# A graph transformer layer on one core: four moves at the seam between its two passes

## What is computed

```python
xn = layernorm(x)
# graph part: per edge an attention over 4 heads; node n takes the transformed row of dst[n]
xt    = xn @ weight                                   # 12500 x 256
alpha = softmax(leaky_relu(xt[src] . attn_l + xt[dst] . attn_r))   # per head
gnn   = sum_h alpha[n, h] * xt[dst[n], h]             # 64 values, repeated for 4 heads
# linear attention: K needs sums over ALL nodes before any message
Q, K  = elu(xn @ Wq) + 1, elu(xn @ Wk) + 1
msg   = layernorm(((Q @ (K^T V)) / (Q @ sum(K))) @ Wm) * g1 + b1
h     = relu(concat(xn, msg) @ W1) @ W2
x     = x + gnn + xn + layernorm(h) * g2 + b2
z     = layernorm(x)                                  # then a shared MLP and 4 experts, top 2
x     = x + shared(z) + gated_experts(z)
```

## Time and profile before

| | |
|---|---|
| median of 3 runs | 1385.67 us |
| lowest and highest | 1385.67 and 1386.52 us |
| the profiled execution | 1385.64 us, of which the span of the trace is 1383.9 us |
| mean granted TensorE clock | 0.993 |
| PE, DVE, POOL, ACT busy | 97%, 76%, 68%, 57% of the span |

### The profile page before, as it was taken

One profiled execution on the slowest core, in us unless ns is written; L12 is line 12 of the kernel. 1 busy time (PEld: TensorE's weight loads), 2 busy tenths in 40 slices (PEclk: granted clock), 3 DMA queues, 4 the chain that ended last, 5 costly groups with the idle time before them and its releaser, 6 DMA issues.

```text
span 1383.9 us, 27085 instructions
## 1 busy us (share of the span) xinstructions
PE 1342.4 (97%) x9032; PEld 1192.8 (86%) x9032; DVE 1049.1 (76%) x2617; ACT 791.4 (57%) x1439; POOL 943.2 (68%) x867
## 2 busy tenths in 40 slices
PE   5999999978999999999999999999999999999998
PEld 4999999866888888888888888888888888888876
DVE  6877777878787777877778777787777877788774
ACT  4555556335655656556565565555665566655565
POOL 4777766758766776677766777667766677667650
PEclk9999999989999999999999999999999999999999
DMA  5787767322212222112211122111221112212000
GB/s 166 254 272 240 241 213 248 116 58 65 68 32 60 69 75 67 30 52 75 75 58 40 53 75 73 44 52 55 75 71 41 56 56 75 71 31 67 4 16 30
DMA packets 71784, 121.81 MB, mean 88 GB/s; under 512 B 38082, under 2 KB 42815, under 8 KB 71752
## 3 DMA queue, kind: packets, MB, share of 16 engines
q1 hardware_dynamic: 55752, 108.00, 24.7%
q0 software_dynamic: 16000, 13.43, 4.5%
HBM read 69.47 MB, written 51.70 MB: 88 GB/s over the span
## 4 chain that ended last, share of the span: by engine, by line
PE 90%; DVE 3%; POOL 2%; issue 1%; DVEq 1%; ACT 1%; POOLq 1%; DMA 1%; SPq 0%; ACTq 0%
PE psum L228 27%; PE psum L229 27%; PE psum L230 27%; PE psum L438 5%; PE psum L518 1%; PE psum L511 1%; PE psum L608 1%; PE psum L707 1%; PE psum L692 1%; POOL xg L1788 1%; POOL ag L1790 1%; DVE base L1445 0%; DMA attn_bc<-in_L_gnn_attn_l 0%; POOL e_lo L1794 0%; POOLq L1727 0%
## 5 line engine op out<-in xcount | busy, mean ns | idle before, releaser
L228 PE MATMUL psum<-w_hi,h_hi 128*125 128x256 f32 x600 | 170.7, 285 | 0.6 <-DVE h_lo L1564 0.5
L230 PE MATMUL psum<-w_hi,h_lo 128*125 128x256 f32 x600 | 168.4, 281 | 0.0
L229 PE MATMUL psum<-w_lo,h_hi 128*125 128x256 f32 x600 | 168.2, 280 | 0.0
L1794 POOL TENSOR_TENSOR h_lo<-relu,h_hi 128x1000 fp32r<-128x1000 f32 x50 | 124.7, 2494 | 49.4 <-ACT h_hi L969 49.3
L1788 POOL DMA_INDIRECT xg<-table_xt,idx x100 | 125.0, 1250 | 39.4 <-issue 38.2
L1790 POOL DMA_INDIRECT ag<-table_al,idx x100 | 122.7, 1227 | 30.5 <-issue 30.5
L228 PE MATMUL psum<-z_hi,w_hi 128*128 128x500 f32 x300 | 121.5, 405 | 1.9 <-DVE z_lo L1573 1.0
L893 ACT ACTIVATE row_n<-psum,nm_m,rs_m 125x256 f32<-125x256 f32 x100 | 48.4, 564 | 127.4 <-POOL nm_m L1730 127.4
L228 PE MATMUL psum<-xT_hi,w_hi 128*128 128x500 f32 x300 | 120.3, 401 | 0.0
L229 PE MATMUL psum<-xT_lo,w_hi 128*128 128x500 f32 x300 | 117.4, 391 | 0.0
L230 PE MATMUL psum<-xT_hi,w_lo 128*128 128x500 f32 x300 | 117.1, 390 | 0.0
(11 more groups left out here) (273 smaller groups left out, 4613.2 us busy)
## 6 DMA issues: line engine op xcount, KB each, us to landing
xb<-in_x SPq DMA_DIRECT2D x50, 448.0 KB
xT_hi_table<-x1T_hi SPq DMA_DIRECT2D x25, 500.0 KB
xT_lo_table<-x1T_lo SPq DMA_DIRECT2D x25, 500.0 KB
xT_hi<-xT_hi_table SPq DMA_DIRECT2D x25, 500.0 KB, 3.9
xT_lo<-xT_lo_table SPq DMA_DIRECT2D x25, 500.0 KB, 4.8
table_xt<-xts SPq DMA_DIRECT2D x25, 455.0 KB
out<-xmid SPq DMA_DIRECT2D x24, 448.0 KB
xb<-in_x SPq DMA_DIRECT2D x50, 52.0 KB
```

Of the source, the lines that this page charges most:

```text
L228: pe.matmul(out, wh, xh, start=first, stop=False)
L229: pe.matmul(out, wh, xl, start=False, stop=False)
L230: return pe.matmul(out, wl, xh, start=False, stop=last)
L1794: ptt(out, src, hi, ALU.subtract).then_inc(S[done], 1)
```

## The change

Four moves, and a new order of tiles in memory that makes one of them legal:

1. DVE: `feature_high(0, 2)` comes after the copy of the key sums.
2. DVE: `second_parts(2)` moves from turn 0 (ahead of `soft_chain_in`) to turn 1 (behind `soft_chain_out`). It reads `w_raw`, memory of pass 1, so the tiles on that memory are now ones that pass 2 writes first in its turn 2 (`e1_hi`, `s2_hi`), and no longer `scaleT`, `mT_hi`, `mT_lo`.
3. POOL: in turn 1 `rstd` of y comes before the first gather of group 2, and `rstd` of z before the second.
4. PE: in turn 2 the two `w1_part` on the x of group 1 come ahead of the wait for `y` and the message's transposes, behind a wait for `m_norm` of group 1.

```diff
@@ tiles @@
-        scaleT = sb("scaleT", [P, GR], F32R)
-        mT_hi = sb("mT_hi", [P, CK, GR], F32R)
-        mT_lo = sb("mT_lo", [P, CK, GR], F32R)
+        e1_hi = sb("e1_hi", [P, 4, GR], F32R)
+        s2_hi = sb("s2_hi", [P, GR], F32R)
...
@@ PE, phase2 @@
+                def hidden_of_old_x():
+                    if x_ahead:
+                        pe.wait_ge(S["m_norm"], T * i)
+                    w1_part(0, 2, 6, xT_old)
+                    w1_part(0, 3, 7, xT_old).then_inc(S["xT_free"], 1)
...
                 if b:
 
+                    if x_ahead:
+                        hidden_of_old_x()
                     if due(i - 1):
                         pe.wait_ge(S["y"], i - 1)
                     transposes(row_n, 0, "mt", "m_norm", T * (i - 1))
-                    w1_part(0, 2, 6, xT_old)
-                    w1_part(0, 3, 7, xT_old).then_inc(S["xT_free"], 1)
+                    if not x_ahead:
+                        hidden_of_old_x()
...
-            phase2(2, 0, own_q=False)
+            phase2(2, 0, own_q=False, x_ahead=True)
@@ DVE, end of pass 1 @@
-            feature_high(0, 2)
             dve.wait_ge(S["hb_mm"], 1)
             dve.memset(kden[:], 0.0)
             dve.wait_ge(S["kx"], NG)
             dve.tensor_copy(kx[:], psum[:, 6:8, 0:KX_W]).then_inc(S["kxs"], 1)
+            feature_high(0, 2)
             dve.drain()
@@ DVE, turn0 and turn1 @@
                 feature_high(1, 2)
-                second_parts(2)
                 dve.drain().then_inc(S["p1_dve"], 1)
...
                 soft_chain_out(0, True, False)
+                second_parts(2)
                 over_den(1, 2)
@@ POOL, turn1 @@
                 rstd(LM, "mv_m", 2, "rs_m")
+                rstd(LY, "mv_y", 1, "rs_y")
                 pool.wait_ge(S["gnn"], 1)
                 pool.wait_ge(S["idx0"], 2 * dma16(2, 0))
                 gathers(0, (0,))
-                rstd(LY, "mv_y", 1, "rs_y")
+                rstd(LZ, "mv_z", 1, "rs_z")
                 gathers(0, (1,))
-                rstd(LZ, "mv_z", 1, "rs_z")
```

More of the change, by code:

```diff
@@ L187, in gps_layer @@
         s1_lo = sb("s1_lo", [P, 2, GR], F32R)
-        e1_hi = sb("e1_hi", [P, 4, GR], F32R)
+        scaleT = sb("scaleT", [P, GR], F32R)
+        mT_hi = sb("mT_hi", [P, CK, GR], F32R)
+        mT_lo = sb("mT_lo", [P, CK, GR], F32R)
         e1_lo = sb("e1_lo", [P, 4, GR], F32R)
-        s2_hi = sb("s2_hi", [P, GR], F32R)
         s2_lo = sb("s2_lo", [P, GR], F32R)
@@ L592, in w2_pair, with phase2 @@
                 last.then_inc(S["w2"], 1)
-            def phase2(i, par, a=True, b=True, c=True, own_q=True):
+            def phase2(i, par, a=True, b=True, c=True, own_q=True, x_ahead=False):
                 xT, mT, zT = (xT_hi[par], xT_lo[par]), (mT_hi, mT_lo), (z_hi, z_lo)
```

## The result

The changed kernel takes 1387.14 us (median of 22 runs, 1385.32 to 1389.80), the kernel before 1385.60 us beside it (22 runs). The ratio is 1.0015, 95% interval 1.0009 to 1.0021: slower by 1.5 us, and above the range that was given. By the bound that the prediction set for telling a change (0.2%) this is "same", on the slow side. One of the 22 executions of the kernel before took 4651.87 us, which nothing here explains and which the median does not feel.

The account below looks back on a forecast made before the run. PE, busy 97% of the span, bounds the kernel, so only its waits can be won; -1.9 (parts 1 to 3) and +0.95 (parts 4 to 6) make -0.95, 1384.7 us, range 1382.8 to 1386.3 us.

Parts of the forecast that it names:

- part 6: POOL, turn 2: six indirect DMAs behind z's root delay h_lo, softmax and rdenT at L518; +0.95 us, bounds -1.2 to +1.3.
- part 3: PE, W1 of turn 1: clock rises at 283.7, 2.9 us behind the restart; message's half 1.9 us earlier, other end -0.4.
- part 5: PE, turn 2: W1 on x first, already hidden before; clock taken as down at message's half; bounds -1.8 to +0.5 us.
- parts 4 to 6: Turn 2 up to L518: gains of parts 4 and 5 swallowed by POOL's later softmax; together +0.95 us.
- Part 1: DVE, end of pass 1: key sums copied 0.7 us earlier, L511 0.4 later; +0.2 us taken, between 0 and 0.4.
- Part 2: Subtraction moved to DVE's gap in turn 1: rs_m takes 1.04 us for 2.15, -1.1 us towards the transposes.
- Part 4: POOL, y's root ahead of the gather: xmid starts at 311.2, behind DVE's memset, not 312.93; -1.7 us, bound -1.2.
- Rival B: Last turns, 1349 to 1352 us: program 1 us earlier, clock fall stays out, 1.6 us more, 1383.1 us; chance 0.22.

Follow-up runs that it names:

- the ten products: Changed kernel plus ten 500-column matmuls into free PSUM bank 7 on PE ahead of L518 of turn 2: 1386.78 us, ratio 1.0008.
- the repaired order: Changed kernel with both pairs of gathers of group 2 ahead of the root of z on POOL: 1384.97 us, ratio 0.9995.
- tiles and split: Kernel before with the new tile order and the last weight's low half (second_parts(2)) a turn later, nothing else: 1386.13 us, ratio 0.9998.

## Why the prediction was wrong

Two steps failed: the layout, put at nothing without a reason, and the end of part 6.

**The order of the tiles was not in the sum.** The prediction costs four moves and not the layout that makes one of them legal. It is worth +1.2 us in the 21 turns of the changed kernel, and 2.5 us by the medians of the run with the tiles alone, of which 1.0 us is in its 21 turns. How the layout slows the products stays open.

**Part 6 stopped at the wait.** The size of the wait was nearly right: +0.95 predicted between the second and third L518, +1.2 measured. How DVE is held was wrong: L1350's counterpart was to slip through at 333.2 and two later ones to be held; in fact it came 0.5 us too late for the gap and was held through `s_lo` and `base`, 4.29 us at one stroke. The gather had been put at some 4 us from issue to landing; it released DVE 6.3 us behind its issue, where it took 4.8 before. Beside it the loads of the next x ran, two of 500 KB, which began at 328.6 us here and at 334.1 in the kernel before. They begin that early in all four kernels with the long wait, and in these alone DVE is done with its own `base` before POOL's `h_lo` starts; whether the loads delay the gather no run separates. For L518 it matters little what is held: in the kernel with the ten products the addition took 0.16 us, and the last operation of the softmax still came 47.7 us behind the L518 of turn 1, as in the changed kernel. And the step ended at PE's wait: that a wait grown from 1.2 to 2.8 us brings the clock down for the six microseconds behind it, +2.8 us, stood in no part and no rival, though part 3 and part 5 reckon with just that at the two waits ahead. POOL's order alone shows it (+1.9 us where parts 4 to 6 gave +0.95; 46.04 us for the turn behind), and the ten products take it away (43.55 us), though the medians show little of that.

**Part 1** had L511 0.4 us later. From the copy of the key sums to L511 it is 2.33 us for 1.53, and the copy itself came 0.7 earlier as worked out, so L511 lost 0.1. The key sums alone gave -0.6 us, which with the +0.2 lies inside what the runs can tell. **Part 2** was right, and is shown: `rs_m` takes 1.05 us for the 2.15 of the earlier trace rows, the moved subtraction lies in DVE's gap and L1647 still waits 1.79 us for PE.

```profile
280.04 1.05 POOL L1734 TENSOR_TENSOR rs_m<-veps_m,neg_half 125x4 f32<-125x4 f32 x1 [1.15 <-issue]
...
287.16 2.03 DVE L1312 TENSOR_TENSOR w_lo<-w_raw,w_hi 128x1792 fp32r<-128x1792 f32 x1
...
290.97 1.26 DVE L1647 TENSOR_TENSOR qf<-qf,psum 128x500 f32<-128x500 f32 x2 [1.79 <-PE psum L518]
```

**Part 3** was right in its size and wrong in its picture. From the first to the second L518 it is 20.79 us for 22.66, -1.9 as predicted. But the level did not rise at 283.7; the 2.9 us from restart to rise were also less than either restart that was read, the shorter being 3.2 us (by the earlier trace rows the level is back at 317.9, not 317.7). In the kernel before it was low from 280.3 to 287.1 us, 6.8 us; in the changed one it fell only at 283.1 and was up at 286.5. The gain is above all a fall that came later, not a rise that came earlier. Two kernels without the split had the short stretch too, so that the sum came out here is in part luck.

**Part 4** was right: `xmid` starts directly behind the memset at 311.05 us. **Part 5** was right that the clock would be down at the message's half (0.50 from 318 to 320 us); what it cost in the repaired order was 0.9 us in the rows (1.2 by the medians) behind L518, where the prediction had PE no longer wait, and nothing in the changed kernel, where L518 waits long either way.

```profile
310.66 0.47 DVE L1700 MEMSET scaleT<- 128x500 f32 x1
311.05 1.53 DVE L1703 SCALAR_TENSOR_TENSOR xmid<-psum,rs_y,g_bc 125x256 f32<-125x256 f32 x4
...
317.76 0.78 PE L228 MATMUL psum<-mT_hi,w_hi 128*128 128x500 f32 x1 [4.04 <-DVE mT_lo L1479]
```

**Rival B** came true in its number, -1.5 us in the profile, and hid a part of the two misses, but by luck: it was to come of the program being 1 us earlier, and the changed one came there 5 us later. The waits for `e_lo` at the end are 3.0 us in two pieces in all eighteen profiles, and the clock fell behind them in six and not in twelve; earliness alone does not decide it, since the key sums' run had its last L518 earliest of all and fell. What does, stays open, as do the 1.5 us of the tiles' run outside its turns.

The account of the whole, from the medians against before: tiles and split +0.1, key sums -0.6, POOL's order +1.9, W1 ahead -0.3 while L518 waits long anyway. That makes +1.1, and +1.5 was measured; each term is known to some 1.2 us only.

## What to carry to other kernels

Cost the layout too: when tiles change places, compare the length of a steady turn between a build with the new order alone and the old one before judging what the order makes legal. Where a wait on the tensor engine grows, price the clock behind it as well as the wait, and ask of every gather pushed behind something else which gap between large operations its consumer was going through. A move of work into a hole is only a gain if the work it leaves behind doesn't meet a lowered clock. And when a wait becomes short, look for what stands right behind it: here a wait of 0.5 us in place of 1.2 to 1.6 made the next turn 1.0 us longer.

## What the runs showed that was not expected

- The same instructions with five tiles in another order in memory: 43.54 to 43.55, 43.58 to 43.60, 43.61, 43.64 and 43.68 us a turn, with PE busy throughout and the clock granted in full.
- A 16-column addition on DVE took 4.29, 4.14 and 1.93 us, each time until one of POOL's large operations with two inputs was over. The Trainium skill (SBUF — State Buffer, SBUF: two separate sides) has the port pair of DVE and GpSimd held by whichever starts first for the whole instruction; here the holder changed from `s_lo` to `base` without letting the waiting addition in.
- A wait of 1.6 us at L518 left the clock up (two kernels); with waits of 2.69 to 2.77 us it was down for 3.4 us (one kernel) or 6.8 us (three). Shown is that the two go together, not from which length on.
- The clock also fell at the end of pass 1 in eleven of eighteen profiles, and in the last turn in six, whatever the edit. From L511 to the first L518 it took 4.5 to 4.7 us where it had fallen, and 3.9 to 4.0 where not.
